# Zeroing of the expert buffer, three early scatters and one key projection, moved in a fused Perceiver block

## The reference, cut to what matters

```python
x = x + xattn(layernorm(x), ctx)      # 2 x 512 queries, 2 x 8192 keys, 16 heads of 32
x = x + attn(layernorm(x))            # 1024 tokens viewed as 2 x 512, causal, amplitude and phase
x = x + moe(layernorm(x))             # 16 experts, top 2, 64 places per expert and batch
...
def _dispatch(xb, pb, cap):
    top_k_probs, ei = jax.lax.top_k(pb, K)
    flat = ei.swapaxes(0, 1).ravel()             # all first choices, then all second choices
    one_hot = jax.nn.one_hot(flat, E)
    pos = jnp.cumsum(one_hot, axis=0) * one_hot  # the place of a token with its expert
    ...
    buf = jnp.zeros((E, cap, C))
    buf = buf.at[ei2.ravel(), pos.ravel()].set(xr, mode='drop')
```

## Time and profile before

| what | value |
|---|---|
| median of 3 runs | 2008.05 us (2007.75 to 2009.68) |
| the profiled execution, its own time | 2003.64 us |
| its span | 2001.9 us |
| PE busy | 1887.0 us, 94% of the span |
| DVE busy | 1705.4 us, 85% |
| ACT busy | 1468.3 us, 73% |
| POOL busy | 45.4 us, 2% |
| mean granted clock of PE | 0.982 |

### The profile page before, as it was taken

One profiled execution on the slowest core, in us unless ns is written; L12 is line 12 of the kernel. 1 busy time (PEld: TensorE's weight loads), 2 busy tenths in 40 slices (PEclk: granted clock), 3 DMA queues, 4 the chain that ended last, 5 costly groups with the idle time before them and its releaser, 6 DMA issues.

```text
span 2001.9 us, 31200 instructions
## 1 busy us (share of the span) xinstructions
PE 1887.0 (94%) x11838; PEld 779.8 (39%) x11838; DVE 1705.4 (85%) x1500; ACT 1468.3 (73%) x1671; POOL 45.4 (2%) x57
## 2 busy tenths in 40 slices
PE   7899999999999999999999999999999989997593
PEld 3333333333333333333333333333332446555582
DVE  5699999999999999979999999999996587876354
ACT  2488888888888888878888888888886456563120
POOL 2000000000000000000000000000000000001103
PEclk9999999999999999999999999999999989999797
DMA  7433322333333333322223333333241000007574
GB/s 247 169 105 90 102 79 79 85 90 90 90 89 91 90 90 95 106 80 80 79 80 90 90 87 93 90 88 97 64 123 47 23 1 1 1 1 264 207 263 151
DMA packets 113354, 194.58 MB, mean 97 GB/s; under 512 B 10288, under 2 KB 64560, under 8 KB 113200
## 3 DMA queue, kind: packets, MB, share of 16 engines
q1 hardware_dynamic: 110640, 184.12, 31.1%
q0 software_dynamic: 2560, 8.39, 1.2%
HBM read 109.63 MB, written 50.33 MB: 80 GB/s over the span
## 4 chain that ended last, share of the span: by engine, by line
PE 84%; DVE 7%; issue 3%; ACT 2%; DMA 2%; POOL 1%; SPq 1%; another core or an unknown queue 0%; POOLq 0%; DVEq 0%; ACTq 0%
PE ps L1105 23%; PE ps L1292 22%; PE ps L1016 12%; PE ps L1019 12%; PE ps L1351 3%; PE ps L1143 2%; PE ps L1138 2%; PE ps L1089 1%; PE ps L1042 1%; PE ps L1361 1%; PE ps L1182 1%; DVE dacc L1723 1%; PE ps L1152 1%; POOL og L988 1%; PE ps L1212 1%
## 5 line engine op out<-in xcount | busy, mean ns | idle before, releaser
L1555 ACT ACTIVATE pt<-ps,bias 128x1024 f32<-128x1024 f32 x1024 | 1108.8, 1115 | 209.4 <-PE ps L1292 207.1
L1723 DVE TENSOR_TENSOR dacc<-dacc,pt 128x2048 f32<-128x2048 f32 x496 | 1134.6, 2287 | 59.0 <-ACT pt L1555 35.0
L1292 PE MATMUL ps<-qst,kst 128*128 128x512 f16 x2048 | 611.2, 381 | 10.8 <-ACT pt L1555 9.9
L1105 PE MATMUL ps<-pt,vt 128*32 128x512 f32 x4096 | 494.5, 599 | 0.0
L1292 PEld LDWEIGHTS ps<-qst,kst 128*128 128x128 f16 x2048 | 177.9, 98 | 416.0 <-ACT pt L1555 126.3
L1016 PE MATMUL ps<-wsm 128*128 128x512 f16 x1152 | 312.4, 382 | 10.7 <-DVE wsm L1681 10.7
L1019 PE MATMUL ps<-wsm 128*128 128x512 f16 x1152 | 309.7, 379 | 2.4 <-ACT vt L1406 2.4
L1105 PEld LDWEIGHTS ps<-pt,vt 128*32 128x32 f32 x4096 | 106.9, 109 | 263.7 <-issue 241.2
L1016 PEld LDWEIGHTS ps<-wsm 128*128 128x128 f16 x1152 | 113.1, 98 | 150.0 <-DVE wsm L1681 10.7
L1019 PEld LDWEIGHTS ps<-wsm 128*128 128x128 f16 x1152 | 112.5, 98 | 140.2 <-ACT vt L1406 2.9
L1666 DVE SCALAR_TENSOR_TENSOR wsm<-ps,wsm 128x512 f16<-128x512 f32 x128 | 87.7, 686 | 33.5 <-ACT wsm L1402 33.5
(11 more groups left out here) (204 smaller groups left out, 1192.8 us busy)
## 6 DMA issues: line engine op xcount, KB each, us to landing
kst<-kscr SPq DMA_DIRECT2D x132, 256.0 KB, 3.5
kscr<-wsm SPq DMA_DIRECT2D x128, 256.0 KB, 3.5
kst<-kst SPq DMA_DIRECT2D x124, 256.0 KB, 3.4
wsm<-in_ctx SPq DMA_DIRECT2D x32, 768.0 KB, 4.8
qst<-qscr SPq DMA_DIRECT2D x32, 128.0 KB, 3.0
xbuf<-xn SPq DMA_DIRECT2D x16, 256.0 KB, 6.3
wsm<-in_gate SPq DMA_DIRECT2D x8, 512.0 KB
wsm<-in_fc SPq DMA_DIRECT2D x8, 512.0 KB
```

Of the source, the lines that this page charges most:

```text
L1105: p = e.matmul(ps[32 * h:32 * h + 32, 4 + n % 2, :], vt[:, kb % 2, ch, c:c + 32], pt[:, (2 * i + h // 2) % 6, h % 2, :], start=ch == 0, st ...
L1292: p = e.matmul(ps[:, 2 * half + h2, :], kst[:, kb % 2, h, ch * 128:ch * 128 + 128], qst[:, h, :], start=True, stop=True)
L1555: e.activation(pt[:, (2 * i + half) % 6], ps[:, 2 * half:2 * half + 2, :], ACT.Exp, bias=bias[:, 4 * kb + ch:4 * kb + ch + 1], scale=SCORE ...
L1723: e.tensor_tensor(own_heads, own_heads, probs, ALU.add).then_inc(S["add"], 1)
```

## The change

It has three parts.

1. The 16 transfers of zeros leave their place ahead of SP's loop. One of them is issued at every eighth step (`i % 8 == 6`) of key blocks 2 to 9, ahead of what SP issues for that step.
2. `unit(1, 0)`, the first unit of the second key block, leaves the first two steps of PE's loop. Six of its nine matmuls are issued ahead of the small matmul L1072, three behind L1074.
3. For tiles 4, 5 and 6 the first choice is made on its own: `rank` and `first` of these three tiles follow the logit of tile 6, and three new pieces, `cumE` (PE, 6 matmuls), `placeE` and `rowsE` (DVE, six instructions), follow the last pair of heads and stand ahead of the last `woT`. Their destinations are `diuE`; POOL scatters these three as soon as they are there. At the end `rank` and `first` run for tile 7 alone, `second`, `cum`, `place` and `rows` for all four tiles as before, and POOL scatters the other five.

```diff
+    def ahead_of_last():
+        out.append(("cumE", 1, fill((2,))))
+        out.append(("placeE", 1))
+        out.append(("rowsE", 1))
...
             slot(a, k)
+            if p == 63:
+                out.append(("rank", 1))
+                out.append(("first", 1))
...
+        ahead_of_last()
         out.append(("woT", 7, 0, 3, (("prob", 63),)))
         out.append(("valueT", 31))
         out.append(("normT", 31))
         out.append(("woT", 7, 3, 4, ()))
...
-    for what in ("rank", "odds", "first", "second"):
-        out.append((what, 1))
+    for what in ("rank", 2), ("odds", 1), ("first", 2), ("second", 1):
+        out.append(what)
...
+CHOSEN = (slice(0, 4), slice(4, 7), slice(7, 8))
...
             e.wait_ge(S["bias"], 2)
-            for i in range(16):
-                e.dma_start(xbuf[128 * i:128 * i + 128, :], att[:, 0, :]).then_inc(S["zero"], 16)
             for i in range(STEPS):
                 kb, g, ch = i // 16, i // 4 % 4, i % 4
+                if i % 8 == 6 and 2 <= kb < 10:
+                    x = i // 8 - 4
+                    e.dma_start(xbuf[128 * x:128 * x + 128, :], att[:, 0, :]).then_inc(S["zero"], 16)
                 if i % 16 == 0 and kb < 30:
                     ctx_load(kb + 2)
...
+            e.wait_ge(S["dst"], 1)
+            for k in range(2):
+                for t in range(4):
+                    scatter(diu[:, k, t:t + 1], t)
+            e.wait_ge(S["dst"], 2)
+            for t in range(4, 7):
+                scatter(diuE[:, t - 4:t - 3], t)
+            e.wait_ge(S["dst"], 3)
+            for k, t in ((0, 7), (1, 4), (1, 5), (1, 6), (1, 7)):
+                scatter(diu[:, k, t:t + 1], t)
...
+            at = bank((1, 0))
+            unit(1, 0, 0, 6, at)
             e.wait_ge(S["maxs"], 5)
             e.matmul(ps[0:1, 0, 0:128], mx[:, 4:5], ident[:], start=True, stop=True).then_inc(S["max1"], 1)
             e.wait_ge(S["maxs"], 6)
             e.matmul(ps[:, 0, 0:1], ones[0:1, :], mx[0:1, 5:6], start=True, stop=True).then_inc(S["max1"], 1)
+            unit(1, 0, 6, 9, at)
...
+                elif what == "cumE":
+                    e.wait_ge(S["ohb"], 2)
+                    for x in range(3):
+                        for q in range(x + 1):
+                            p = e.matmul(ps[:, 2, 128 + 16 * x:144 + 16 * x], (trib if q == x else onesb)[:],
+                                         ohb[:, 0, 4 + q], start=q == 0, stop=q == x)
+                    p.then_inc(S["cum"], 1)
...
-                    if n < 3 and kb < 31:
+                    if n < 3 and kb < 31 and i > 1:
```

More of the change, by code:

```diff
@@ L621, in self_order @@
         follow(7, step)
-    for what in ("rank", "odds", "first", "second"):
-        out.append((what, 1))
+    if kept:
+        out.append(("rank", 1))
+        out.append(("first", 1))
+        ahead_of_last()
+    for what in ("rank", 2), ("odds", 1), ("first", 2), ("second", 1):
+        out.append(what)
     out.append(("cum", 1, 5, ()))
@@ L742, in build @@
         diu = sb("diu", [128, 2, 8], U32)
+        diuE = sb("diuE", [128, 3], U32)
         s3 = ExitStack()
@@ L977, in pool, with scatter @@
             e.wait_ge(S["zero"], 256)
[L978 to L983, removed]
+            def scatter(rows, t):
+                e.indirect_dma_start(out=xbuf, out_offset=bass.IndirectOffsetOnAxis(ap=rows, axis=0),
+                                     in_=xn3[:, t, :], in_offset=None).then_inc(S["sct0"], 16)
+            e.wait_ge(S["dst"], 1)
[8 more added lines that the diff above has]
+                scatter(diu[:, k, t:t + 1], t)
             e.wait_ge(S["ciu"], 2)
@@ L1115, in self_piece @@
                 what, t = ev[0], ev[1]
-                if what in ("turn", "p01", "p23", "p4", "qkT", "wo", "woT", "rT", "router", "colsum", "score", "scoreT", "cum", "pT"):
+                if what in ("turn", "p01", "p23", "p4", "qkT", "wo", "woT", "rT", "router", "colsum", "score", "scoreT", "cum", "cumE", "pT"):
                     for name, value in ev[-1]:
@@ L1271, in self_piece @@
                     b, bank_ = t, ev[2]
-                    e.wait_ge(S["ohb"], b + 1)
+                    e.wait_ge(S["ohb"], 2 * b + 1)
                     for x in range(8):
@@ L1533, in self_piece @@
                 elif what == "odds":
-                    e.wait_ge(S["lgs"], t + 1)
+                    e.wait_ge(S["lgs"], 2 * t + 1)
                     e.activation(pp[:, 4 * t:4 * t + 4], lg[:, 4 * t:4 * t + 4], ACT.Exp).then_inc(S["pexp"], 1)
@@ L1765, in wide @@
             def wide(ap, n=16):
-                return ap.unsqueeze(2).to_broadcast([128, 4, n])
+                return ap.unsqueeze(2).to_broadcast([128, ap.shape[1], n])
             squared = 0
@@ L1913, in self_piece @@
                 elif what == "rank":
-                    tiles = slice(4 * t, 4 * t + 4)
-                    e.wait_ge(S["lg"], 4 * t + 5)
+                    tiles = CHOSEN[t]
+                    e.wait_ge(S["lg"], tiles.stop + 1)
                     e.tensor_reduce(v8[:, tiles], lg[:, tiles], AX.X, ALU.max).then_inc(S["dve"], 1)
@@ L1919, in self_piece @@
                 elif what in ("first", "second"):
-                    tiles, k = slice(4 * t, 4 * t + 4), 0 if what == "first" else 1
-                    back = iot[:, 1, :].unsqueeze(1).to_broadcast([128, 4, 16])
+                    tiles, k = (CHOSEN[t], 0) if what == "first" else (slice(4 * t, 4 * t + 4), 1)
+                    back = iot[:, 1, :].unsqueeze(1).to_broadcast([128, tiles.stop - tiles.start, 16])
                     e.wait_ge(S["const"], 1)
@@ L1940, in self_piece @@
                     mark = e.tensor_tensor(ohb[:, k, tiles], wide(ei[:, k, tiles]), back, ALU.is_equal)
-                    if k:
+                    if k or t == 1:
                         mark.then_inc(S["ohb"], 1)
@@ L1959, in self_piece @@
                     counts = ps[:, ev[2], 128:256].rearrange("p (k t n) -> p k t n", k=2, n=16)
-                    e.wait_ge(S["cum"], t + 1)
+                    e.wait_ge(S["cum"], 2 * t + 1)
                     e.tensor_tensor(w3[:].rearrange("p (k t) n -> p k t n", k=2), counts, ohb[:, :, 4 * t:4 * t + 4, :],
@@ L1964, in self_piece @@
                     tiles = slice(4 * t, 4 * t + 4)
-                    e.wait_ge(S["cumr"], t + 1)
+                    e.wait_ge(S["cumr"], 2 * t + 1)
                     e.tensor_reduce(po[:, :, tiles], w3[:].rearrange("p (k t) n -> p k t n", k=2), AX.X,
@@ L1979, in self_piece @@
                     e.tensor_copy(ciu[:, :, tiles], ci[:, :, tiles]).then_inc(S["ciu"], 1)
+                elif what == "placeE":
+                    e.wait_ge(S["cum"], 2)
+                    e.tensor_tensor(w3[:, 0:3], ps[:, 2, 128:176].rearrange("p (t n) -> p t n", n=16), ohb[:, 0, 4:7, :],
+                                    ALU.mult).then_inc(S["cumr"], 1)
+                elif what == "rowsE":
+                    e.wait_ge(S["cumr"], 2)
+                    e.tensor_reduce(po[:, 0, 4:7], w3[:, 0:3], AX.X, ALU.add).then_inc(S["dve"], 1)
+                    e.wait_ge(S["dve"], own.up())
+                    e.scalar_tensor_tensor(out=dr[:, 0, 4:7], in0=po[:, 0, 4:7], scalar=64.5, in1=tro[:, 0, 4:7],
+                                           op0=ALU.is_ge, op1=ALU.mult).then_inc(S["dve"], 1)
+                    e.wait_ge(S["dve"], own.up())
+                    e.tensor_scalar(po[:, 0, 4:7], po[:, 0, 4:7], 64.0, 12863.0, ALU.min, ALU.add).then_inc(S["dve"], 1)
+                    e.wait_ge(S["dve"], own.up())
+                    e.scalar_tensor_tensor(out=ci[:, 0, 4:7], in0=ei[:, 0, 4:7], scalar=128.0, in1=po[:, 0, 4:7],
+                                           op0=ALU.mult, op1=ALU.add).then_inc(S["dve"], 1)
+                    e.wait_ge(S["dve"], own.up())
+                    e.tensor_tensor(diuE[:], ci[:, 0, 4:7], dr[:, 0, 4:7], ALU.max).then_inc(S["dst"], 1)
             for i in range(STEPS):
```

## The result

Beside the kernel before, the changed kernel took 1994.74 us (median of 4 runs, 1991.70 to 1996.82) against 2008.82 (4 runs): ratio 0.9929, 95% interval 0.9912 to 0.9946. The gain is 14.1 us, between 10.8 and 17.7.

What follows compares the result with a forecast made beforehand. PE, busy 94% of the span, was taken as the bound, so only its idle stretches could give time. 5.31 + 0.16 + 4.0, say 9.5 us, off the 2008.05 median gave 1998.6 us; range 1996.5 to 2000.5, 8-in-10 range 1995.0 to 2003.0.

Steps and rivals of the forecast that it cites:

- 5.31 + 0.16: Start of cross-attention: 5.31 us from removing the waits for key stores (part 1), 0.16 us from the moved unit (part 2).
- forecast 77.9: First key store to `kscr`: SP issues it at about 77.9 us, and it lands 3.5 us later.
- The step that sized part 2: First pair of steps: 1.94 us of matmuls leave it, but ACT's exponentials set the pace, so only 0.16 us is gained.
- my row for 68 to 72 us: Profile window where the scores' bound is made: PE busy only 1.21 us yet at clock 1.00, used against a clock fall.
- a rival in which the change makes the clock fall: First pair of steps: short new idle pieces lower PE's clock, losing 5.6 us, time 2004.2; chance 3%.
- The cost of the zeros: Key blocks 2 to 9: spread zeros cost nothing, since SP has 15.8 us free for two issues per block.
- The slower rival: Key blocks: zeros hold up the keys; from 0.84 us of PE each, over 0.2% slower; 2014.6 at 1 us; chance 3%.
- I take 4.0, with 3.6 as the lower end: Final scatters: three of eight leave the end, 3.79 us, plus 0.2 us from smaller DVE instructions.
- the three scatters cost nothing: Self-attention's end: the early scatters run 10 us before the five others start and don't delay them.
- the early scatters give nothing: Rival at the end: the last landing sets the end, or the three hold up the five; 2002.6 us; chance 5%.
- everything behind shifts: Experts after the scatters: their first matmuls wait only for the `xbuf` load, so the 4.0 us gain carries through.
- 2008.05 - 9.5: Whole kernel: the summed gain of 9.5 us taken off the median of the runs, giving 1998.6 us.

Runs made afterwards that it cites:

- e8: Part 1 plus nine matmuls with thrown-away results where part 2 puts the unit, which stays in the loop, against the kernel before: ratio 0.9967.
- e2: Part 1 alone (zeros issued in blocks 2 to 9) against the kernel before, chip A: ratio 0.9977.
- e7: Parts 1 and 3, with the unit left in the loop, against the kernel before, chip B: ratio 0.9953.
- e4: Part 3 alone (early choice and three early scatters) against the kernel before, chip A: ratio 0.9991.
- e14: Part 3 alone again, on chip D, against the kernel before: ratio 0.9999.
- e15: Part 3 alone, but POOL issues the three early scatters only when the last rows are known, against the kernel before, chip D: ratio 0.9997.
- e1: The kernel before, unchanged, compared with itself as a control, chip A: ratio 0.9994.
- e9: Part 3 alone again, on chip C, against the kernel before: ratio 0.9998.
- e12: The kernel before with 24 zero transfers ahead of the loop in place of 16, against the kernel before, chip C: ratio 1.0026.
- e11: The whole change with 32 spread zero transfers in place of 16, against the kernel before, chip C: ratio 0.9965.
- e6: Parts 1 and 2, without the early scatters, against the kernel before, chip B: ratio 0.9965.
- e5: The whole change once more, on chip B, against the kernel before: ratio 0.9937.
- e18: The whole change once more, on chip E, against the kernel before: ratio 0.9956, median 1999.49 us.
- e3: Part 2 alone (unit (1, 0) ahead of the loop) against the kernel before, chip A: ratio 0.9994.
- run 10: The whole change with 80 useless matmuls ahead of the experts' first transposes, against the kernel before, chip C: ratio 0.9979.
- e17: The whole change, with the three early scatters held until PE's last router product, against the kernel before, chip E: ratio 0.9942, median 1996.59 us.
- e13: The whole change a third time, on chip D, against the kernel before: ratio 0.9968.

## Why the prediction was too small

**Part 1 and 2, the head: right as a sum, 5.67 us for 5.31 + 0.16; its split holds only while PE keeps its clock.** The stores came as forecast: issued at 77.44 (forecast 77.9), landed within 2.95 us (3.5); no ACT wait for `kscr`, the clock at 1.00, no sign of DVE being late. With the clock kept by the filler, part 1 is worth 5.30 us for 5.31 (e8), and the work moved 0.36 for 0.16. But part 1 alone took 3.6 us off the head in e2 (2.6 in e7, beside part 3), and part 2 adds 2.05 to 3.03, not 0.16. The step that sized part 2 asked only whether 1.94 us of matmuls leave the pair. It missed that without them PE's clock can fall: my row for 68 to 72 us said busy 1.21 us and clock 1.00, in one execution, and I took this for a rule. Of the nine traces of kernels with nothing in the pause, five (e2, e4, e7, e14, e15) have 0.57 to 0.79 in the window 70 to 78 us and four (before, e1, e9, e12) have 1.00; with the unit or the filler in it, all have 1.00. The Trainium skill, page "TensorE: Matmul & The Clock Gate", section "A second HAM failure mode: psum-queue depth-cycling", was cited for a rival in which the change makes the clock fall. A clock that falls behind short pauses is in these traces, but in kernels without part 2. With part 2 PE does pause for 0.83 and 0.40 us between score pairs, as forecast, and in none of the ten traces with it did the clock fall: for this change the traces don't agree with that rule. What the change takes away are the longer pauses ahead of step 0.

**The cost of the zeros: nothing, as said.** e11 shows it with twice their number. The slower rival (from 0.84 us each) is out. Ahead of the loop they cost 0.65 us each by the times, 0.76 by the traces.

**Part 3: "I take 4.0, with 3.6 as the lower end" is a mis-sized term.** Between the two profiles it measured 61.61 - 56.05 = 5.56 us. Between e6 and e5, on one chip, it is 4.02, as worked out; and on chips A, C and D about nothing (e18 on chip E has the same long stretch, 62.07). The step that failed there is that the three scatters cost nothing because they lie 10 us ahead of the five. They do not delay the five directly; where the wait occurs, they delay the last reciprocal by 2.46 us (e14 against e15) and what is behind it by 1.40 more, on a PE that then runs at a lower clock. The rival "the early scatters give nothing" (5%) was right in its outcome on those chips: the five are indeed held up by something that the three started, but through PE's results and not in GpSimd's queue. The kernel before has such a wait too, a smaller one, behind its first eight scatters:

```profile
1816.38 0.96 POOL L982 DMA_INDIRECT xbuf<-xn,diu  x1 [0.30 <-issue]
...
1818.12 0.96 DVE L1880 RECIPROCAL pr<-ps 128x128 f32<-128x128 f32 x1 [1.22 <-remote]
```

I had read past this line of before's trace. The changed kernel's profile has no such wait there. That is part of the 1.5 us by which 5.56 is above 4.0: in the kernels with before's end, the stretch is 61.6 to 61.8 us where this wait occurs (before, e1, e2, e3, e12) and 61.2 where it doesn't (e6, e8). The rest is within what one and the same kernel shows: 56.05 in the changed kernel's profile, 57.14 in e5.

**The sum against the time: the step that put the forecast outside.** In the traces the terms came out near their sizes. The two stretches give 5.67 + 5.56 = 11.2 us between the first two profiles, and 5.67 + 4.02 = 9.7 on chip B, for 9.5 forecast. The medians moved by 14.1 and, on chip B, by 12.6 (9.8 to 15.5), both times 2.9 us more. So what failed is "everything behind shifts", with "2008.05 - 9.5": a sum read from one execution was taken off a median, as if the change left all else, and the mix of executions, as it was. It didn't. The forecast for the profiled execution was 1994.1, and it took 1996.82, too slow by 2.7 us, because 4.7 of the 11.2 were given back elsewhere in that pair of traces: 1.1 in the cross-attention behind the head, 1.6 in the self-attention stretch, 1.9 behind the last scatter.

The record of the single executions shows where to look for the 2.9 us. Two of the changed kernel's four ran at a mean granted clock of 0.984 and took 1991.70 and 1993.13 us; the two at 0.981 took 1996.36 and 1996.82. None of the 107 executions of the kernel before that ran beside e1 to e18 is above 0.982. In the four kernels whose traces have the scatters in less than 59 us (changed, e5, e7, e17), 7 of 21 executions have 0.983 or 0.984, and each time they are the fastest of their kernel; in all others without extra matmuls at the experts it is 1 of 228. Without them the gain would be 12.2 us beside the sum of 11.2, and on chip B 10.5 beside 9.7. That a shorter stretch of scatters lets PE keep or regain its clock in some executions fits this, but it is not shown: none of the seven was profiled, and in which stretch their clock is higher stays open.

The range failed for the same reason: I gave it the bounds of the parts, and no room for executions unlike the profiled one, nor for a part that is worth 0 to 5.6 us depending on the chip. The self-attention stretch alone takes from 248.7 (e13) to 254.8 us (e6) in single executions whose code differs there in little. And it would have been luck had the changed kernel first run on chip D or E: its 2000.76 and 1999.49 us lie inside the range, with a part 3 that gives nothing in its stretch.

**What stays open.** What differs between the chips. All eight traces with the early issue on A, C, D and E show the wait of 4.6 us, the three others (the changed kernel's own, e5, e7 on chip B) do not. The small wait behind the first group goes with it: before's own trace and all fourteen on A, C, D and E have it, those of chip B and the changed kernel's own have not. In e14, e15 and e17 the profile names PE in place of "remote" as what ended it, but the size and the place are the same:

```profile
1817.92 0.96 POOL L998 DMA_INDIRECT xbuf<-xn,diu  x1 [0.30 <-issue]
...
1819.69 0.96 DVE L1914 RECIPROCAL pr<-ps 128x128 f32<-128x128 f32 x1 [1.26 <-PE ps L1228]
```

So the small wait, which is in the trace of the kernel before, tells whether the early issue will meet the large one. Each chip was used in one session only, so that chip and session are not told apart; and as before's profile has the small wait and the changed kernel's has not, these two may come from different chips. Whether it is the writing of descriptors, a fetch of instructions, or the handing on of a semaphore that is held up was not told apart; e15 and e17 show that the moment of POOL's issuing decides. That the placing of code plays a part was not tried.

## What to carry to other kernels

Look at the granted clock behind every pause of PE that lies next to a wait you mean to remove, in more than one trace: the wait may hide a slow stretch that then comes out, and useful work put into the pause can be worth more than its own length (2.05 to 3.03 us for 1.94 here). Work moved onto GpSimd "beside" others isn't free because its queue is empty: ask who waits for a result of PE until a microsecond behind its last scatter, and issue it where nobody does. Make a forecast from the stretches that change, and give its range the spread between chips and executions as well as the bounds of the parts. A sum from one execution is a forecast for that execution; look at the clock and time of all the others before you take it off their median.

## What the runs showed of the hardware

With three indirect scatters on GpSimd, a result of PE that was ready at 1848.56 was used by DVE at 1850.51, 0.88 us behind the last of them; in the eight traces of this kind the distance is 0.85 to 0.96 us and the wait 4.62 to 4.73 us; behind the group of eight, in fifteen traces, 0.75 to 0.90 and 1.20 to 1.35 us. ScalarE is held up beside it: in the same fifteen traces its next read of PE's scores starts 0.88 to 1.03 us behind the eighth scatter, after a wait of 2.60 to 2.75 us; in the five without the small wait it starts about 0.6 us before that scatter ends, after 1.12 us. The Trainium skill, page "DMA: Bandwidth & Descriptors", section "SWDGE vs HWDGE vs iDMA", tells of the other direction, VectorE locking GpSimd out while it generates descriptors; here it is PE's result that comes late behind GpSimd, and no run shows whether the two are related.

Nine matmuls of 0.215 us in PE's pauses of 2.8 us together kept the granted clock of the next 8 us at 1.00 in all eleven traces that have them (ten with the useful ones, one with useless ones, e8); without them it fell in five of nine traces, to between 0.57 and 0.79.
